# First attention's front rebuilt, its level products made block by block, and the second FFN added straight into the output

## The chip, the cores and the metric

The program runs on one core of a Trainium2 chip. A core has five engines that run side by side and meet only at semaphores: TensorE (PE), VectorE (DVE), ScalarE (ACT), GpSimd (POOL) and SyncE (SP, which only issues transfers here). The metric is the time of one execution in microseconds, smaller being better. The kernel before takes 764.98 us (median of three runs, 763.76 to 766.53).

## The reference

`x` is 2 sequences of 2048 tokens by 128 features, all in float32. Four sublayers follow each other, each added to `x` and each reading the layer-normalised `x`: attention a, an FFN, attention b, the same FFN again.

```python
# attention a (what the change is about)
V = complex(mat_v_real, mat_v_imag)           # 64 x 64
Vinv = inv(V)
a2 = (xf @ w_a.T).reshape(b, l, 64, 2)        # complex pair
a  = a2 as complex * rsqrt(mag2) * sigmoid(log(mag2))
xc = (xf @ w_x.T) as complex * sqrt(mag2)
u  = einsum('mn,bln->blm', Vinv, x_roll)      # x_roll: h0, then xc shifted by one
s  = associative_scan of (a, a * u) along l   # s_t = a_t * (s_{t-1} + u_t)
h  = einsum('mn,bln->blm', V, s) + xc
y  = h.real @ w_out.T
# FFN: each of 16 experts takes its 256 best tokens (top_k over tokens)
xe = xn[idx];  h = gelu(xe @ fc1.T + b1);  y = h @ fc2.T + b2
output = zeros.at[flat_idx].add(y * gates);   output / gate_sums
```

## The kernel before, in words

Everything is written by hand: each engine has its own instruction list and semaphores are counted, so the order on an engine is the order of the code.

**Front of attention a.** The tokens are worked in four blocks `k` of 512 tokens of both sequences. SP loads the four 64x64 parts of `V` and its transpose (eight loads), then the eight groups of `x`, then the weights. DVE makes the statistics of all tokens, ACT one square root (`root(0)`, L470), and then, block by block: DVE normalises into `stage` (L969; two groups, reused, so block k+1 waits for the transposes of block k), PE transposes into PSUM, ACT copies to `xT` (L474, `keep_xT`), PE projects with `waT` into four PSUM banks (L689), ACT squares the four banks (L501), copies them to `av` and `XC` (L507, L508) and takes the square root of the magnitudes (L513). DVE's `coefficients(k)` adds the squares (L1009, `mag`), takes `1/(1+mag)` (L1011, L1012) and scales `XC` and `av` (three products, by the helper at L934).

**The inverse.** `inv(V)` comes from a Newton iteration on the real 128x128 form of `V`, with 24 steps of two links: link one is PE L662 and L664 and ACT L484 (`Zm`), link two PE L668 and L669 and ACT L488 (both copies of `XX`). `inverse(n)` emits links up to number n; calls of it are woven into the blocks on PE and ACT (eight links a block), and the rest follow the last block. DVE then builds `BD` from the result (L1034 to L1039) and prepares bit masks for later (`bits`, ten tiny steps by L934 and L938).

**The scan.** PE makes `u` in five chunks (L709 to L712), DVE folds each chunk with `av` (`U_CHUNKS`), and then goes up and down the ten levels of a tree. The products of coefficients of each level, `lev`, are made by POOL (L385 to L388, four instructions a level) once all of `av` is there (`proj_used` at `NK`); DVE waits for them by `lev_ready`. PE multiplies the result by the output weights (L720), DVE adds it to `x`.

**The FFN** (`feed(f)`, run twice). After the choice of tokens, POOL issues indirect transfers: gathers of an expert's 256 rows from `tab` into the ring `XE` of eight places (L415, two a gather), and scatters of `y` that add into DRAM (L431, two an expert). Seven experts are gathered ahead. Even experts add into `acc[f][0]`, which holds a copy of `x`, odd ones into `acc[f][1]`, which SP has zeroed (L291). A scatter waits for the one two experts before it. DVE makes `y` (L1234, L1237) and waits ahead of it (L1232) for the same scatter. At the end SP reads both arrays back (L314, L318), DVE and POOL add them (L438) and in the second FFN SP stores the sum to `out` (L329).

Of the kernel before, what the change touches and what calls it, by code (L numbers as in the profile page):

```python
# [14 lines left out]
P = 128  # L15
# [22 lines left out]
def build(nc, x, wa, wx, wo, vr, vi, vrT, viT, h0r, h0i, wqkvT, woutT, nw, rwT, rb, f1T, f1b, f2T, f2b, out):  # L38
# [26 lines left out]
    acc = [[nc.dram_tensor(f"acc{f}{i}", [NTOK, D], F32).ap() for i in range(2)] for f in range(2)]  # L65
    cntd = [nc.dram_tensor(f"cntd{f}", [P, GW], F32).ap() for f in range(2)]

    with ExitStack() as ctx:
# [25 lines left out]
        aI = sb("aI", [P, 2, P])  # L94
# [10 lines left out]
        SS = carve(2 * LT).rearrange("p (c t) -> p c t", c=2)  # L105
        XC = carve(2 * (LT + 1)).rearrange("p (c t) -> p c t", c=2)
# [52 lines left out]
        RX = 8  # L159
        XE = carve(RX * 2 * TW).rearrange("p (r h w) -> p r h w", r=RX, h=2)  # L160
# [46 lines left out]
        scattered = [sem(f"scattered{i}") for i in range(2)]  # L207
        acc_in = [sem(f"acc_in{g}") for g in range(NG)]
# [18 lines left out]
        stored = sem("stored")  # L227
# [5 lines left out]
        nw_start, nw_sq, nw_norm, nw_Y, nw_Z, nw_X, nw_new, nw_newT = (sem(s) for s in ("nw_start", "nw_sq", "nw_norm", "nw_Y", "nw_Z", "nw_X", "nw_new", "nw_newT"))  # L233
# [6 lines left out]
        N_WIDE, N_LAST = 18, 6  # L240
        HALVES = 2 * (N_WIDE + N_LAST)
# [4 lines left out]
        WA, WB = 3.5, 3.5 * 3.5 / 4  # L246

# [8 lines left out]

        @block.sync
        def _(sp):
            for t, src in ((RT[0:64, 0:64], vrT), (RT[64:128, 64:128], vrT), (RT[0:64, 64:128], viT), (RT[64:128, 0:64], viT),
                           (Rm[0:64, 0:64], vr), (Rm[64:128, 64:128], vr), (Rm[0:64, 64:128], vi), (Rm[64:128, 0:64], vi)):  # L260
                sp.dma_start(t, src).then_inc(inv_in, 16)
            for g in [b * NK + k for k in range(NK) for b in range(NB)]:
                b, k = divmod(g, NK)
                sp.dma_start(xs[:, g * TPG:(g + 1) * TPG, :],
                             x[b, k * GW:(k + 1) * GW, :].rearrange("(t p) d -> p t d", p=P)).then_inc(x_in[g], 16)
# [23 lines left out]
            for f in range(2):  # L289
                for g in range(NG):  # L290
                    sp.dma_start(acc[f][1][g * GW:(g + 1) * GW, :].rearrange("(p r) w -> p (r w)", r=TPG), zero  # L291
                                 ).then_inc(zeroed, 16)

            def feed(f):
# [4 lines left out]
                for g in range(NG):  # L299
                    sp.dma_start(acc[f][0][g * GW:(g + 1) * GW, :].rearrange("(t p) w -> p t w", p=P),  # L300
                                 xs[:, g * TPG:(g + 1) * TPG, :]).then_inc(base_in, 16)
# [10 lines left out]
                sp.wait_ge(scattered[0], 32 * NE // 2 * (f + 1))  # L312
                for g in range(NG):
                    sp.dma_start(xs[:, g * TPG:(g + 1) * TPG, :], acc[f][0][g * GW:(g + 1) * GW, :].rearrange("(t p) w -> p t w", p=P)  # L314
                                 ).then_inc(acc_in[g], 16)
                sp.wait_ge(scattered[1], 32 * NE // 2 * (f + 1))
                for g in range(NG):
                    sp.dma_start(acc1[:, g * TPG:(g + 1) * TPG, :], acc[f][1][g * GW:(g + 1) * GW, :].rearrange("(t p) w -> p t w", p=P)  # L318
                                 ).then_inc(acc_in[g], 16)
# [3 lines left out]
            for g in range(NG):  # L323
                b, k = divmod(g, NK)
                if g % 2:
                    sp.wait_ge(x_ready_pool, HALF_NG + g // 2 + 1)
                else:
                    sp.wait_ge(x_ready, HALF_NG + g // 2 + 1)
                sp.dma_start(out[b, k * GW:(k + 1) * GW, :].rearrange("(t p) d -> p t d", p=P),  # L329
                             xs[:, g * TPG:(g + 1) * TPG, :]).then_inc(stored, 16)  # L330
            sp.wait_ge(stored, 16 * NG)

        @block.gpsimd
        def _(pool):
# [39 lines left out]
            pool.wait_ge(proj_used, NK)  # L374
            pool.wait_ge(projected, NK)
            lo = 0
            A = av
            for lv in range(1, LEVELS):
                n = LT >> lv
                B = lev[:, :, lo:lo + n]  # L380
                lo += n
                t1 = xT[:, 0:2 * n].rearrange("p (c t) -> p c t", c=2)
                t2 = xT[:, 2 * n:4 * n].rearrange("p (c t) -> p c t", c=2)
# [3 lines left out]
                pool.tensor_tensor(B[:, 0, :], t1[:, 0, :], t2[:, 1, :], ALU.subtract).then_inc(lev_ready, 1)  # L387
                pool.tensor_tensor(B[:, 1, :], t1[:, 1, :], t2[:, 0, :], ALU.add).then_inc(lev_ready, 1)  # L388
                pool.wait_ge(lev_ready, 2 * lv)
                A = B  # L390

            def feed(f):

                pool.wait_ge(zeroed, 16 * NG * 2)
# [13 lines left out]
                def gather(e):  # L408
                    if e == 0:
                        pool.wait_ge(idx_ready, f + 1)  # L410
                    if e >= RX:
                        pool.wait_ge(y_ready, f * NE + e - RX + 1)
                    for h in range(2):
                        i = h * NE + e
                        pool.indirect_dma_start(out=XE[:, e % RX, h, :], out_offset=None, in_=tab[f],  # L415
                                                in_offset=bass.IndirectOffsetOnAxis(ap=idx[:, i:i + 1], axis=0)
                                                ).then_inc(xe_in[e % RX], 16)

                for e in range(RX - 1):
                    gather(e)  # L420
                pool.wait_ge(base_in, 16 * NG * (f + 1))
                for e in range(NE):
                    if e + RX - 1 < NE:
                        gather(e + RX - 1)
                    pool.wait_ge(y_ready, f * NE + e + 1)
                    if f * NE + e >= 2:

                        pool.wait_ge(scattered[e % 2], 32 * ((f * NE + e) // 2))
                    for h in range(2):
                        i = h * NE + e  # L430
                        pool.indirect_dma_start(out=acc[f][e % 2], out_offset=bass.IndirectOffsetOnAxis(ap=idx[:, i:i + 1], axis=0),  # L431
                                                in_=yv[:, e % 2, h, :], in_offset=None, compute_op=ALU.add
                                                ).then_inc(scattered[e % 2], 16)

                for g in range(1, NG, 2):
                    t = slice(g * TPG, (g + 1) * TPG)
                    pool.wait_ge(acc_in[g], 32 * (f + 1))
# [25 lines left out]
        def _(act):  # L463

# [7 lines left out]
            def keep_xT(run, n, g):  # L472
                act.wait_ge(transposed, run * NG + n + 1)
                nc.scalar.activation(xT[:, g * GW:(g + 1) * GW], ps[:, 6 + n % 2, :], ACT.Copy).then_inc(xT_ready, 1)  # L474
# [3 lines left out]
            def inverse(upto):  # L478

                while done[0] < min(upto, HALVES):  # L480
                    i, half = divmod(done[0], 2)
                    if half == 0:
                        act.wait_ge(nw_Y, i + 1)
                        nc.scalar.activation(Zm[:, :], ps[:, 5, 0:P], ACT.Copy).then_inc(nw_Z, 1)  # L484
                    else:
                        act.wait_ge(nw_X, i + 1)
                        for a, ready in enumerate((nw_new, nw_newT)):
# [7 lines left out]
            def squares(k, at):  # L495
                inverse(at + 5)
                act.wait_ge(projected, k + 1)
                if k >= 1:
                    act.wait_ge(mag_ready, k)
# [878 lines left out]
```

## Time and profile before

| quantity | value |
|---|---|
| median of 3 runs | 764.98 us |
| the profiled execution | 773.48 us, its span 771.7 us |
| DVE busy | 471.5 us, 61% of the span |
| PE busy | 434.5 us, 56% |
| POOL busy | 347.9 us, 45% |
| ACT busy | 208.8 us, 27% |
| first attention | 0 to about 192 us |
| second FFN's gathers, experts and end | about 644 us to the end |

No engine is busy all the time: the stages have different limits, and each is read by itself. In the timeline a row gives the start in us, the length in us, the engine, the line of the program, what is written and read, and in brackets how long the engine had been idle and what ended that. In the chain of waits a row is a piece of the one path that ended last. In windows of time an engine's number is its busy time in us, and PEclk is the granted share of TensorE's clock. "Landing" is the time from the issue of a transfer to its completion.

### The profile page before, as it was taken

The page shows a single profiled execution, that of the slowest core. Times are in us where ns is not written, and L with a number is a line of the kernel's source. Part 1 is how long each engine was busy: PE and PEld are TensorE (multiplying, and loading weights), DVE is VectorE, ACT ScalarE, POOL GpSimd, SP SyncE. Part 2 cuts the span into 40 slices and gives each one's busy share as a digit, 9 for nine tenths or more (in the row PEclk, how much of TensorE's full clock was granted, in tenths as well). Part 3 has the DMA queues.
Part 4 walks back from the last instruction along what each step waited for, and adds up shares of the span by engine and source line. Part 5 has one row for each costly group of instructions (what it writes and reads, how often), then busy time and mean ns, then how long its engine had stood idle before and what let it go on. Part 6 is the DMA issues. An engine that isn't in the chain of part 4 may idle for free.

```text
span 771.7 us, 7616 instructions
## 1 busy us (share of the span) xinstructions
PE 434.5 (56%) x2146; PEld 289.0 (37%) x2146; DVE 471.5 (61%) x1205; ACT 208.8 (27%) x511; POOL 347.9 (45%) x330
## 2 busy tenths in 40 slices
PE   4787476008432157778007889888753313887730
PEld 3544344007211056667003334334331102776630
DVE  5475699999777712222066898999967883221211
ACT  2547100000443013223026333323143401232210
POOL 5000790000100066888425877787810004688872
PEclk9999568658855578999558888998976555889975
DMA  4790000000500522333730000000050014233359
GB/s 128 265 400 8 0 0 1 0 0 7 157 0 0 148 52 37 45 45 37 159 79 0 0 1 1 0 1 0 1 163 2 0 47 133 44 45 44 36 84 277
DMA packets 63684, 47.30 MB, mean 61 GB/s; under 512 B 9184, under 2 KB 58976, under 8 KB 62368
## 3 DMA queue, kind: packets, MB, share of 16 engines
q1 hardware_dynamic: 52256, 37.81, 16.1%
q0 software_dynamic: 11392, 9.05, 8.8%
q8 instruction: 17, 0.28, 0.1%
q14 instruction: 19, 0.16, 0.1%
HBM read 26.92 MB, written 19.92 MB: 61 GB/s over the span
## 4 chain that ended last, share of the span: by engine, by line
DVE 24%; POOL 24%; issue 18%; PE 13%; DMA 9%; ACT 5%; SPq 3%; another core or an unknown queue 1%; DVEq 1%; POOLq 0%
POOL acc L431 9%; DVE arena L934 8%; POOL tb L459 8%; DMA acc<-arena,idx 5%; POOL arena L415 4%; DVE tk L939 2%; PE ps L720 2%; DVE arena L939 2%; PE ps L689 2%; DVE tb L969 2%; DMA tab<-tb 2%; PE ps L768 1%; DMA arena<-acc 1%; POOL arena L455 1%
## 5 line engine op out<-in xcount | busy, mean ns | idle before, releaser
L431 POOL DMA_INDIRECT acc<-arena,idx x64 | 101.2, 1581 | 27.6 <-issue 16.2
L934 DVE TENSOR_TENSOR arena<-ps,arena 128x256 f32<-128x256 f32 (+1 forms) x36 | 16.3, 453 | 138.0 <-DMA acc<-arena,idx 115.4
L549 ACT ACTIVATE arena<-ps,b 128x256 f32<-128x256 f32 x128 | 50.1, 474 | 148.1 <-PE ps L820 115.8
L820 PE MATMUL ps<-arena,f1w 128*128 128x256 f32 x256 | 74.5, 442 | 27.7 <-DVE arena L938 23.1
L459 POOL TENSOR_TENSOR tb<-arena 128x512 f32<-128x512 f32 x64 | 80.5, 1271 | 17.0 <-DVE arena L1296 17.0
L867 PE MATMUL ps<-xT,arena 128*128 128x512 f32 x128 | 72.3, 660 | 20.3 <-DVE arena L1296 20.2
L415 POOL DMA_INDIRECT arena<-tab,idx x64 | 62.4, 975 | 41.8 <-DMA tab<-tb 22.9
L830 PE MATMUL ps<-f2w,arena 128*128 128x128 f32 x512 | 68.5, 287 | 7.1 <-issue 7.0
L830 PEld LDWEIGHTS ps<-f2w,arena 128*128 128x128 f32 x512 | 67.4, 203 | 10.7 <-issue 8.1
L820 PEld LDWEIGHTS ps<-arena,f1w 128*128 128x128 f32 x256 | 54.1, 222 | 39.9 <-DVE arena L938 26.9
L934 DVE TENSOR_TENSOR arena<-arena 128x256 f32<-128x256 f32 (+26 forms) x127 | 56.4, 479 | 2.6
L254 POOL DMA_DIRECT2D arena<-cntd x4 | 2.7, 687 | 117.0 <-DMA cntd<-arena 117.0
L720 PE MATMUL ps<-tb,arena 128*128 128x256 f32 x96 | 25.2, 430 | 43.8 <-DVE arena L934 37.8
L385 POOL TENSOR_TENSOR xT<-arena 128x2048 f32<-128x2048 f32 (+9 forms) x10 | 10.7, 1075 | 69.1 <-DVE arena L934 68.4
L396 POOL CAST arena<-ident 128x128 f16<-128x128 f32 x2 | 0.6, 290 | 89.6 <-DVE tb L969 89.6
L939 DVE TENSOR_SCALAR_CACHE_REDUCE arena<-arena,tk 128x320 f16<-128x320 f32 (+1 forms) x66 | 37.1, 564 | 4.7 <-DVE tk L939 2.1
L867 PEld LDWEIGHTS ps<-xT,arena 128*128 128x128 f32 x128 | 22.6, 207 | 44.6 <-DVE arena L1296 36.5
L720 PEld LDWEIGHTS ps<-tb,arena 128*128 128x128 f32 x96 | 20.9, 220 | 48.6 <-DVE arena L934 38.2
L470 ACT ACTIVATE sd<-sd 128x32 f32<-128x32 f32 x4 | 0.9, 229 | 140.6 <-DVE sd L957 140.6
L538 ACT ACTIVATE arena<-arena,tk 128x192 f16<-128x192 f32 x60 | 27.3, 455 | 41.8 <-DVE tk L939 39.6
L1296 DVE TENSOR_TENSOR_SCAN arena<-ones,arena,ps 128x512 f32<-128x512 f32 x30 | 37.3, 1260 | 0.0
L455 POOL TENSOR_TENSOR arena<-arena 128x512 f32<-128x512 f32 x24 | 30.5, 1272 | 8.7 <-ACT arena L608 8.6
(220 smaller groups left out, 948.1 us busy)
## 6 DMA issues: line engine op xcount, KB each, us to landing
tab<-tb SPq DMA_DIRECT2D x8, 576.0 KB, 5.7
f1w<-in_f1T SPq DMA_DIRECT2D x4, 1024.0 KB, 11.0
f2w<-in_f2T SPq DMA_DIRECT2D x4, 1024.0 KB, 13.0
acc<-tb SPq DMA_DIRECT2D x16, 256.0 KB, 12.1
acc<-xs SPq DMA_DIRECT2D x16, 256.0 KB, 6.3
xs<-acc SPq DMA_DIRECT2D x16, 256.0 KB, 5.5
arena<-acc SPq DMA_DIRECT2D x16, 256.0 KB, 5.4
xs<-in_x SPq DMA_DIRECT2D x8, 256.0 KB, 4.9
```

What stands on the lines that cost most here:

```text
L415: pool.indirect_dma_start(out=XE[:, e % RX, h, :], out_offset=None, in_=tab[f], in_offset=bass.IndirectOffsetOnAxis(ap=idx[:, i:i + 1], ax ...
L431: pool.indirect_dma_start(out=acc[f][e % 2], out_offset=bass.IndirectOffsetOnAxis(ap=idx[:, i:i + 1], axis=0), in_=yv[:, e % 2, h, :], in_ ...
L455: pool.tensor_tensor(KV[:, j % 2, :], KV[:, j % 2, :], kn[:, r, :], ALU.mult).then_inc(kv_ready, 1)
L459: pool.tensor_tensor(QS[:, i, :], ST[:, r, i, :], qn[:, r, :], ALU.mult).then_inc(qs_ready, 1)
L549: last = nc.scalar.activation(hT[:, e % 2, t, :], ps[:, 2 * (e % 2) + t // 2, (t % 2) * CAP:(t % 2 + 1) * CAP], ACT.Gelu, bias=b1[:, e, t: ...
L720: return nc.tensor.matmul(ps[:, n, t * 2 * D:(t + 1) * 2 * D], lhs, MB[:, i, :, :].rearrange("p b d -> p (b d)"), start=(i == 2 and t == 0 ...
L820: last = nc.tensor.matmul(ps[:, 2 * (e % 2) + t // 2, (t % 2) * CAP:(t % 2 + 1) * CAP], f1w[:, e, t * P:(t + 1) * P], xeT[:, e % 2, :], st ...
L830: last = nc.tensor.matmul(ps[:, 6 + m % 2, h * P:(h + 1) * P], hT[:, m % 2, t, h * P:(h + 1) * P], f2w[:, m, t, :], start=(t == 0), stop=( ...
L867: nc.tensor.matmul(ps[:, u % V_BANKS, :], WV[:, i, :, :].rearrange("p h a -> p (h a)"), xT[:, n * GW:(n + 1) * GW], start=True, stop=True) ...
L934: return nc.vector.tensor_tensor(o, a, b, op)
L939: return nc.vector.tensor_scalar(o, a, s1, s2, op0, op1, **kw)
L1296: nc.vector.tensor_tensor_scan(ST[:, r, i, :], ones_in.to_broadcast([P, GW]), kv, ST[:, 1 - r, i, GW - 1:GW] if n % NK else 0.0, ALU.mult, ...
```

## The change

- **x on two queues.** ACT issues four of the loads of `V` and the four `x` groups of the first sequence; SP keeps the others. A square root right at the start draws ACT's table load forward. DVE makes the statistics of the first `x` group ahead of the start of the inverse.
- **The front in one go.** All 32 tiles are normalised at once into `XN`, which lies in parts of the arena that are still free, so no block waits for `stage`. The transposes of block k+1 and the squares of block k stand between the projections, the raw copy is made ahead of the squares (which now read SBUF), and all front transposes use bank 7.
- **The inverse in other steps.** Ten pairs of three links (`form`, `square`, `apply`) and two last steps of two links: 34 links, six a block, where there were 48 and eight. The copies into `BD` and `MB` go from DVE to ACT.
- **Level products per block.** POOL makes the first two levels' products of each block when its coefficients are there, the others as before; it waits for `mag_ready` of the next block first.
- **Second FFN into `out`.** `x` is copied to `out`, and all experts of the second FFN add there; each scatter waits for the one just before it. Six experts are gathered ahead instead of seven, and each further gather stands behind a scatter. The reading back, the addition and the store at the end are gone, and so is half of the zeroing.

```diff
-        AT_FIRST, AT_STEP = 7, 8
+        PAIRS = (3.9,) * 8 + (3.4, 2.2)
...
+        AT_ROOT, AT_FIRST, AT_STEP = 8, 12, 6
+
+        BY_BLOCK = 2
...
@@ SP, end of feed(f)
+                if f:
+                    sp.wait_ge(base_in, 16 * NG * 2)
+                    sp.wait_ge(out_scattered, 32 * NE)
+                    return
...
@@ POOL, levels
-            pool.wait_ge(proj_used, NK)
...
+            for k in range(NK):
+
+                pool.wait_ge(proj_used, k + 1)
+                if k + 1 < NK:
+                    pool.wait_ge(mag_ready, k + 2)
+                pool.wait_ge(transposed, min(2 * (k + 2), NG))
+                A = av[:, :, k * GW:(k + 1) * GW]
+                for i in range(BY_BLOCK):
+                    n = GW >> (i + 1)
...
+                    level(A, B, n)
...
@@ POOL, feed(f)
+                def scatter(e):
+                    pool.wait_ge(y_ready, f * NE + e + 1)
+                    if f:
+                        if e:
+                            pool.wait_ge(out_scattered, 32 * e)
...
+                        scatter(e)
+                        for s in range(got, min(got + 2, 2 * NE)):
+                            gather(s)
...
@@ PE, blocks
+                for i in range(2):
...
+                    last.then_inc(projected, 1)
+                    inverse(at + 2 * i + 1)
+                    if k + 1 < NK:
+                        transposes(0, 2 * (k + 1) + i, lambda t: XN[i][k + 1][:, t, :])
+                    inverse(at + 2 * i + 2)
+                inverse(at + 6)
...
@@ DVE
-            norm_a(0)
             for k in range(NK):
-                if k + 1 < NK:
-                    norm_a(k + 1)
+                norm_a(k)
+            for k in range(NK):
                 coefficients(k)
...
-            V.did(nc.vector.tensor_copy(BD[lo_, 0, lo_], XX[lo_, 1, lo_]))
...
```

Three places in the engines' lists. First ACT between the projections of one block and the next (`Zm`, `XX`: the inverse; `arena<-ps 128x2x512`: a raw copy; `tb<-tb`: the square root; `arena<-ps 128x256`: the copy in a pair's middle), before:

```order
L501 ACTIVATE arena<-ps 128x512 x2
L484 ACTIVATE Zm<-ps 128x128
L501 ACTIVATE arena<-ps 128x512 x2
L488 ACTIVATE XX<-ps 128x128 x2
L507 ACTIVATE arena<-ps 128x2x512
L508 ACTIVATE arena<-ps 128x2x512
L484 ACTIVATE Zm<-ps 128x128
L513 ACTIVATE tb<-tb 128x1024
L474 ACTIVATE xT<-ps 128x512
L488 ACTIVATE XX<-ps 128x128 x2
L474 ACTIVATE xT<-ps 128x512
```

The same engine there after the change:

```order
L562 ACTIVATE arena<-ps 128x2x512
L531 ACTIVATE Zm<-ps 128x128
L521 ACTIVATE xT<-ps 128x512
L553 ACTIVATE tb<-tb 128x1024
L569 ACTIVATE arena<-arena 128x1024
L535 ACTIVATE arena<-ps 128x256
L562 ACTIVATE arena<-ps 128x2x512
L539 ACTIVATE XX<-ps 128x128
L541 ACTIVATE XX<-ps 128x128
L521 ACTIVATE xT<-ps 128x512
L569 ACTIVATE arena<-arena 128x1024
```

A raw copy now frees its banks first, and the next block's `xT` stands between the halves of this one. The second place is POOL's first two levels, before:

```order
L385 TENSOR_TENSOR xT<-arena 128x2048 [waits projected,proj_used]
L386 TENSOR_TENSOR xT<-arena 128x2048
L387 TENSOR_TENSOR arena<-xT 128x1024 [waits gstep]
L388 TENSOR_TENSOR arena<-xT 128x1024
L385 TENSOR_TENSOR xT<-arena 128x1024 [waits lev_ready]
L386 TENSOR_TENSOR xT<-arena 128x1024
```

The same work for one of the four blocks after the change:

```order
L395 TENSOR_TENSOR stage<-arena 128x512 [waits mag_ready,proj_used,transposed,lev_ready,gstep]
L396 TENSOR_TENSOR stage<-arena 128x512
L397 TENSOR_TENSOR arena<-stage 128x256 [waits gstep]
L398 TENSOR_TENSOR arena<-stage 128x256
L395 TENSOR_TENSOR stage<-arena 128x256 [waits lev_ready,gstep]
L396 TENSOR_TENSOR stage<-arena 128x256
```

Each block's share is a quarter in size and starts with the block. The third place is POOL's transfers in the second FFN at the first experts, before (`arena<-tab,idx`: half a gather, `acc<-arena,idx`: half a scatter):

```order
L415 DMA arena<-tab,idx 128x144 [waits base_in]
L415 DMA arena<-tab,idx 128x144
L431 DMA acc<-arena,idx 4096x128 [waits scattered0,y_ready]
L431 DMA acc<-arena,idx 4096x128
L415 DMA arena<-tab,idx 128x144 [waits y_ready]
L415 DMA arena<-tab,idx 128x144
L431 DMA acc<-arena,idx 4096x128 [waits scattered1,y_ready]
L431 DMA acc<-arena,idx 4096x128
```

After the change:

```order
L442 DMA arena<-tab,idx 128x144 [waits idx_ready,tab_stored]
L442 DMA arena<-tab,idx 128x144 x11
L455 DMA out<-arena,idx 4096x128 [waits y_ready,base_in]
L455 DMA out<-arena,idx 4096x128
L442 DMA arena<-tab,idx 128x144 x2
L455 DMA out<-arena,idx 4096x128 [waits out_scattered,y_ready]
L455 DMA out<-arena,idx 4096x128
```

Twelve half gathers stand ahead of the first scatter where there were sixteen, and a scatter's wait is now on the one directly before it.

## Rows read from the trace of the kernel before

**Rows 1.** Chain of waits over the span: start us, length us, what.
```profile
25.89 1.87 PE ps L689 x8
...
65.78 1.87 PE ps L689 x8
...
88.53 2.62 DVE BD L1034
...
98.43 2.29 DVE bits L934
```
**Rows 2.** Timeline of the start of the front.
```profile
12.98 0.79 PE L664 MATMUL ps<-XX,RT 128*128 128x128 f32 x2
...
14.14 0.79 PE L668 MATMUL ps<-Zm,XX 128*128 128x128 f32 x2 [0.37 <-ACT Zm L484]
...
15.72 0.79 PE L664 MATMUL ps<-XX,RT 128*128 128x128 f32 x2
...
16.85 1.28 ACT L470 ACT_TABLE_LOAD   x1
...
18.14 0.23 ACT L470 ACTIVATE sd<-sd 128x32 f32<-128x32 f32 x1
```
**Rows 3.** Windows: PE, PEld, DVE, ACT, POOL busy, PEclk, DMA share, GB/s.
```profile
39.00:52.00 13.00, 9.87 (x56) 5.67 (x55) 9.85 (x14) 8.20 (x21) 0.00 (x0) 1.00 1.01 395
...
76.00:88.00 12.00, 10.33 (x36) 7.95 (x36) 6.85 (x8) 3.96 (x14) 5.89 (x2) 0.53 0.00 0
```
**Rows 4.** DVE from 76 to 106 us by shape: busy us, mean ns, idle.
```profile
L1012 DVE RECIPROCAL tb<-tb 128x512 f32<-128x512 f32 x1 | 3.4, 3352 | 0.0
L1034 DVE COPY BD<-XX 64x64 f32<-64x64 f32 x1 | 2.6, 2619 | 5.6 <-ACT XX L488 5.6
L934 DVE TENSOR_TENSOR arena<-arena,tb 128x1024 f32<-128x1024 f32 x2 | 2.5, 1225 | 0.1
...
L1035 DVE COPY BD<-XX 64x64 f32<-64x64 f32 x1 | 0.2, 192 | 0.0
```
**Rows 5.** POOL from 76 to 120 us by shape.
```profile
L385 POOL TENSOR_TENSOR xT<-arena 128x512 f32<-128x512 f32 x1 | 1.3, 1266 | 0.1
...
L387 POOL TENSOR_TENSOR arena<-xT 128x256 f32<-128x256 f32 x1 | 0.7, 727 | 0.1
```
**Rows 6.** Timeline of DVE: the first chunk's fold, and the levels' start.
```profile
105.87 0.75 DVE L934 TENSOR_TENSOR arena<-arena,ps 128x256 f32<-128x256 f32 x2
...
129.04 47.75 DVE L934 TENSOR_TENSOR arena<-arena 128x256 f32<-128x256 f32 x104
```
**Rows 7.** Timeline: last gather ahead and first `y`, in both FFNs.
```profile
290.60 0.94 POOL L415 DMA_INDIRECT arena<-tab,idx  x1 [0.30 <-issue]
...
294.25 0.42 DVE L934 TENSOR_TENSOR arena<-ps,arena 128x256 f32<-128x256 f32 x1 [11.54 <-remote]
...
663.36 0.95 POOL L415 DMA_INDIRECT arena<-tab,idx  x1 [0.30 <-issue]
...
667.03 0.42 DVE L934 TENSOR_TENSOR arena<-ps,arena 128x256 f32<-128x256 f32 x1 [10.98 <-remote]
```
**Rows 8.** Timeline of POOL: first half scatters of two experts, and the last half scatter.
```profile
668.26 1.65 POOL L431 DMA_INDIRECT acc<-arena,idx  x1 [3.95 <-DVE arena L938]
...
674.71 1.63 POOL L431 DMA_INDIRECT acc<-arena,idx  x1 [0.30 <-issue]
...
747.66 1.55 POOL L431 DMA_INDIRECT acc<-arena,idx  x1 [0.30 <-issue]
```
**Rows 9.** Chain of waits from 655 us: from a scatter's issue to its landing.
```profile
689.49 3.30 DMA acc<-arena,idx
...
736.53 4.17 DMA acc<-arena,idx
...
747.66 6.30 DMA acc<-arena,idx
```
**Rows 10.** Timeline of SP: the stores of the result.
```profile
760.49 6.92 SPq L329 DMA_DIRECT2D out<-xs  x8
```

More of the change, by code:

```diff
@@ L64, in build @@
     tab = [nc.dram_tensor(f"tab{f}", [NTOK, TW], F32).ap() for f in range(2)]
-    acc = [[nc.dram_tensor(f"acc{f}{i}", [NTOK, D], F32).ap() for i in range(2)] for f in range(2)]
+    acc = [nc.dram_tensor(f"acc{i}", [NTOK, D], F32).ap() for i in range(2)]
+    outf = out.rearrange("b t d -> (b t) d")
     cntd = [nc.dram_tensor(f"cntd{f}", [P, GW], F32).ap() for f in range(2)]
@@ L322, in _ @@
             feed(1)
[L323 to L331, printed above, removed]
         @block.gpsimd
@@ L419, in feed @@
-                for e in range(RX - 1):
-                    gather(e)
+                        pool.indirect_dma_start(out=outf if f else acc[e % 2],
+                                                out_offset=bass.IndirectOffsetOnAxis(ap=idx[:, i:i + 1], axis=0),
+                                                in_=yv[:, e % 2, h, :], in_offset=None, compute_op=ALU.add
+                                                ).then_inc(out_scattered if f else scattered[e % 2], 16)
+                got = 2 * AHEAD[f]
@@ L421, in feed @@
+                for s in range(got):
+                    gather(s)
                 pool.wait_ge(base_in, 16 * NG * (f + 1))
                 for e in range(NE):
[L423 to L433, printed above, removed]
+                    if f == 0:
+                        for s in range(got, min(got + 2, 2 * NE)):
+                            gather(s)
+                            got += 1
+                        scatter(e)
+                    else:
+                        scatter(e)
+                        for s in range(got, min(got + 2, 2 * NE)):
+                            gather(s)
+                            got += 1
@@ L670, in inverse @@
                     done[0] += 1
+            for b in range(NB):
+                inverse(AT_FIRST - 1 + b)
+                transposes(0, b, lambda t: XN[b][0][:, t, :])
+            pe.wait_ge(wab_in, 32)
             for k in range(NK):
                 at = AT_FIRST + AT_STEP * k
-                for b in range(NB):
-                    inverse(at + b)
-                    if k == 0 and b == 0:
-                        pe.wait_ge(wab_in, 32)
-                    transposes(0, 2 * k + b, lambda t: stage[:, b * TPG + t, :])
```

314 lines of the change are left out of this document (180 added, 134 removed).

## The prediction, made before the changed kernel ran

> **What bounds the kernel now.** I read the chain of waits first, for the places where the end is decided, then the timeline of those two places, then windows and groups by shape for durations. In the front the chain stands on the projections [rows 1]: from 25.89 to 65.78 are three blocks, 13.3 us each. It does not go from there to the scan: it goes over the inverse, whose links run on alone after the last block, to DVE's copies into BD at 88.53, to the bit masks at 98.43, and only at 105.87 does DVE fold the first chunk [rows 6]. From there to about 174 us DVE works without a gap worth naming, so what is won ahead of 105.87 is won for the whole program, since nothing behind it reads a clock. In the second FFN POOL's own issuing is the pace: an expert starts each 6.45 us [rows 8], and POOL's idle time before a scatter is its own 0.30. Then come the landing, the reading back, the sum and the store.
>
> **The front's start: 1.6 us lost.** A Newton step's first link took 1.16 us (12.98 to 14.14) and its second 1.58 (14.14 to 15.72) [rows 2]. A pair of the new kind has a form at 1.16, a square of four products with one wider copy at about 1.65, and an apply at 1.16, since its first product alone releases the next link: 3.97 us. The two queues bring V's parts about 1.8 us sooner, but DVE now makes one group's statistics first and waits for its x, so I let the first link start at 10.4 instead of 9.8. The root stands behind eight links: 10.4 + 2 x 3.97 + 1.16 + 1.65 = 21.15, ending at 21.4, against 18.37 before, although the table load of 1.28 us there is gone [rows 2]. From the root to the first projection it was 7.5 us; with fewer links between, and no wait for stage, I take 6.0: the first projection starts at 27.4 against 25.8.
>
> **The blocks: 6 us won by the last projection.** Per block ACT was busy 8.20 us [rows 3]. Four steps of three copies become two pairs of four, one of them wider: twelve copies of about 0.24 (8.20 us over 21 instructions, the other nine being much longer) against eight of 0.3, so 7.7. The new order makes ACT's list one string: it waits for PE's first projection of the block (1.87, with the wake 2.0) and, at the end, PE waits for the last square and apply (about 1.0). 7.7 + 2.0 + 1.0 = 10.7. Last projection: 27.4 + 3 x 10.7 = 59.5, against 65.8. DVE's part of a block is two products of 1.23, one of 0.68, the sum of 1.23, 0.43 and the reciprocal of 3.35 [rows 4]: 8.2, below 10.7.
>
> **What POOL's blocks cost DVE.** BD's copies of 64x64 took 2.62 us beside a POOL product and 0.19 in a gap between two [rows 4], so DVE stands until POOL's instruction ends. A block's eight POOL instructions are two of 1.27, four of 0.73 and two of about 0.4: 6.2 us; the largest two and the 0.7 are [rows 5], the smallest are an estimate by size. The wait for the next mag keeps the sum of squares free of them and the reciprocal (3.35) covers about half, so the loss a block lies between 0 and 6.2; I take 1.0 to 1.5, most of which the slack of 10.7 - 8.2 swallows in blocks 1 and 2. Only the last block's 0.9 shows. The Trainium skill ("SBUF — State Buffer", on GpSimd and VectorE contention) calls the shared ports an exclusive lock held for the whole instruction, which also binds a product with both inputs in SBUF; the copies agree. By that page every one of the five such instructions of a block could meet a POOL instruction, and the sum would be the third rival's.
>
> **The way to the first chunk.** The last mag comes 8.1 us after the last projection, at 67.6, and av is complete at 67.6 + 8.2 + 0.9 = 76.7 (82.0 before). All 34 links are spent with block 3, so BD is built by ACT near 71, and PE has the first two chunks ready. The whole piece from 82.0 to 98.4, waiting for the inverse and copying BD in POOL's gaps, falls away. What is late next is DVE's own bit masks, 98.43 to 105.87, 7.4 us, mostly waits for POOL: they stay, because POOL starts block 3's products at the same moment. First chunk: 76.7 + 7.4 = 84.1 instead of 105.87, 21.8 us earlier. The folds of the five chunks took 23.2 us (105.87 to 129.04) [rows 6] while POOL finished small levels; now it has larger ones beside them, for which I charge 1.4 (bounds 0 and 4). **Front: 20.4 us won.** Level products are not a wait: from 83 POOL needs some 15 us more, and DVE takes up the levels at 108.6.
>
> **The second FFN, its start.** DVE stood 10.98 us until the first y at 667.03, and the profile names no engine for it ("remote"); in the first FFN it was 11.54 us at the same place [rows 7]. In both FFNs the first y comes 3.65 and 3.67 us after the last gather ahead was issued [rows 7]; though the idle times differ by over 0.5. I read that something these engines need stands behind the gathers. Twelve half gathers instead of sixteen, at 1.25 us each, end the stall 5.0 us earlier, and the first scatter starts at 663.3 instead of 668.3. Bounds: 0 and 5, since no more than the four gathers can be taken out.
>
> **Its pace.** Ten experts still have a gather behind their scatter: 6.43 us. The second half scatter is issued 1.93 us after the first and lands 3.3 to 4.2 us later [rows 9]; 1.93 + 3.4 + 0.3 = 5.65 is hidden under 6.43. For the last six experts it is not hidden: 5.65 instead of 3.7 each (two half scatters at 1.55 + 0.30 [rows 8]). First scatter at s, last one's start at s + 10 x 6.43 + 5 x 5.65 = s + 92.6, its landing at + 1.93 + 3.4 = s + 97.9, that is 761.2 for s = 663.3. The end was 771.7: a last landing of 6.30 us, the reads, the sum and the stores (760.49 + 6.92 and their landing) [rows 9, 10] are gone. **10.3 us won**; serialising alone costs about 10, the end gives back 18.
>
> **Small edits at nothing.** Half the zeroing (under the blocks), x copied to out instead of acc (lands while the choice runs), MB's copies on ACT (after BD, needed by chunk 1 only). If the cover of MB were gone: 1 us.
>
> **Sum.** 20.4 + 10.3 = 30.7. Against the profiled execution's span, 771.7 - 30.7 = 741.0. The profiled execution is 8.5 us above the median of the runs; I take the same difference off the median: 764.98 - 30.7 = 734.3, told as 734.
>
> **Rivals.**
> 1. *The stall is not tied to the gathers* (a fixed wait that begins with the first experts). The first scatter stays at 668.3, the FFN gives 5.3: 739. For it: the gathers start at the same point too, so two equal cases can't part the two. 24%.
> 2. *PE's clock stays at the lower level in the blocks.* In the blocks before, the granted clock was 1.00, and it fell to 0.53 (1.2 GHz of 2.4) when only links ran [rows 3]; the new blocks hold the same products in less time, which speaks against it. With all products at the lengths of 13 us (0.79 where a fast one is about 0.49 by the ratio of the levels), a block's two projections cost 2 x 1.16 more and the links and transposes in its string about 1.1: 4 x 3.4 = 13.6 us: 748. 4%.
> 3. *DVE becomes the bound of the blocks.* All of POOL's 6.2 us fall on it: 14.4 a block instead of 10.7, 3 x 3.7 = 11 us: 745. Against: the reciprocal covers half. 12%.
> 4. *The front starts at full speed.* Denser links bring the quick level before the first transposes: 3.7 us less, 730 or 731. 7%.
> 5. *Slower: every scatter into one array lands as late as the last one.* That one took 6.30 us [rows 9]. Each expert then costs 1.93 + 6.3 + 0.3 = 8.53; 663.3 + 15 x 8.53 + 8.2 = 799.5, 27.8 later than 771.7; with the front's 20.4 that is 772. It decides from a landing of 5.9 us on. Against: nearly all scatters landed in 3.3 to 4.3, and the late one ran beside eight reads of acc. 3%.
>
> My own case has 50%, and its range is 731 to 738. **Range 726 to 747**: down past the fourth rival with both bounds at their good end, up to the third. Within 0.3% (2.3 us) a measurement of this kernel can't tell a change. Faster by more: all but the fifth rival and a remnant, 0.95; within it 0.02; slower 0.03.
>
> **What the profile after would show.** Right: three distances of about 10.7 between first projections; BD written by ACT near 71, before the last coefficients; DVE's first chunk at 84; POOL products of 512 beside each block; the first y of the second FFN at 3.7 us after its twelfth half gather; scatters at 6.4 and then 5.7 us. Wrong: distances above 12 (rivals 2 and 3, told apart by PEclk and by the length of DVE's products of 1.23); a first y that comes 22.5 us after the first gather again (rival 1); waits before scatters while gathers are still left (rival 5).

## The result, and the profile after

The changed kernel takes 736.9 us (median of 4 runs, 735.7 to 738.6) beside 765.8 us of the kernel before in the same session (763.8 to 768.5): a ratio of 0.9623, 95% interval 0.9597 to 0.9649, or 28.8 us less. I had predicted 734 and a gain of 30.7 us, 20.4 in the front and 10.3 in the second FFN. The profiled execution after took 735.7 us, its span is 733.9.

The chain of waits in the front (start, length, what), which answers to [rows 1]:
```profile
24.41 1.94 PE ps L770 x8
...
35.16 1.87 PE ps L770 x8
...
45.85 1.87 PE ps L770 x8
...
56.54 1.89 PE ps L770 x8
...
64.50 1.39 DVE tb L1098
66.37 3.36 DVE tb L1101
69.76 1.49 DVE arena L1021
71.25 1.14 DVE tb L1021
72.42 1.63 DVE arena L1021
75.01 1.18 DVE bits L1021
```
The first projections are 10.7 us apart (13.3 before). The copies into BD have left the chain; only DVE's bit masks stand between the last product of av and the first fold. The links at the start, PE's timeline, against [rows 2]:
```profile
9.52 0.80 PE L731 MATMUL ps<-arena,ident 128*128 128x128 f32 x2 [1.08 <-DVE nrm L1080]
...
12.92 0.80 PE L753 MATMUL ps<-arena 128*128 128x128 f32 x2 [0.47 <-ACT arena L535]
13.51 0.45 PE L754 MATMUL ps<-arena 128*128 128x128 f32 x2
...
14.08 0.49 PE L733 MATMUL ps<-XX,RT 128*128 128x128 f32 x2
...
16.98 0.49 PE L733 MATMUL ps<-XX,RT 128*128 128x128 f32 x2
```
From 13.5 us the same products take 0.39 to 0.49 us instead of 0.63 to 0.80, and a pair of links takes 2.90 us (14.08 to 16.98). The first pair, nearly all of it at the long lengths, took 3.97 (10.11 to 14.08), which is the length I had taken for all of them. DVE's bit masks and folds, and its take-up of the levels, against [rows 6]:
```profile
73.97 0.43 DVE L1021 TENSOR_TENSOR bits<-ione,ish 128x32 uint32<-128x32 uint32 x1
...
74.82 0.15 DVE L1025 TENSOR_SCALAR bits<-bits 128x1 uint32<-128x1 uint32 x1
75.01 1.17 DVE L1021 TENSOR_TENSOR bits<-bits 128x1 uint32<-128x1 uint32 x1
...
78.92 0.75 DVE L1021 TENSOR_TENSOR arena<-arena,ps 128x256 f32<-128x256 f32 x2
...
103.37 2.81 DVE L1021 TENSOR_TENSOR arena<-arena 128x256 f32<-128x256 f32 x3
```
The levels start 25.7 us earlier than in [rows 6]. A mask operation over one element a partition takes 1.17 us and ends with POOL's product of 512 (74.91 to 76.17), where the one before it, with a single input, takes 0.15: most of the 1.17 is a wait. In the second FFN, the first y on DVE and then POOL's last gather ahead, first scatter and last two half scatters ([rows 7, 8]):
```profile
627.83 0.42 DVE L1021 TENSOR_TENSOR arena<-ps,arena 128x256 f32<-128x256 f32 x1 [3.48 <-PE ps L917]
```
```profile
626.68 0.94 POOL L442 DMA_INDIRECT arena<-tab,idx  x1 [0.30 <-issue]
630.21 1.66 POOL L455 DMA_INDIRECT out<-arena,idx  x1 [2.59 <-issue]
...
724.67 1.55 POOL L455 DMA_INDIRECT out<-arena,idx  x1 [2.44 <-DMA out<-arena,idx]
726.53 1.55 POOL L455 DMA_INDIRECT out<-arena,idx  x1 [0.31 <-issue]
```
The first y is worked 1.15 us after the last gather ahead was issued, not 3.65, and DVE waits for PE, no longer for something "remote". The chain at the end shows the serial steps of the last experts, and what follows the last issue:
```profile
714.73 3.34 DMA out<-arena,idx
718.11 0.71 issue
718.83 1.55 POOL out L455
720.37 0.30 issue
720.68 3.24 DMA out<-arena,idx
...
724.67 1.55 POOL out L455
```

### The profile page after: what moved, and what is told of

Read it like the earlier page. It is cut to its first block, busy times and chain, and to the rows that moved or that the text cites. A ratio compares the mean times of both kernels' runs of the same rounds, so it can differ in the third digit from the quotient of the medians.

```text
span 733.9 us, 7537 instructions
## 1 busy us (share of the span) xinstructions
PE 410.8 (56%) x2130; PEld 273.7 (37%) x2130; DVE 461.8 (63%) x1199; ACT 205.2 (28%) x487; POOL 355.6 (48%) x350
## 4 chain that ended last, share of the span: by engine, by line
DVE 27%; POOL 22%; issue 17%; DMA 15%; PE 13%; ACT 4%; SPq 1%; DVEq 1%; ACTq 0%; POOLq 0%
DVE arena L1021 10%; POOL tb L501 8%; DMA out<-arena,idx 5%; DMA acc<-arena,idx 5%; POOL acc L455 4%; POOL out L455 4%; POOL arena L442 3%; DVE tk L1026 2%; PE ps L807 2%; DVE arena L1026 2%; PE ps L770 2%; DVE tb L1056 2%; DMA tab<-tb 2%; PE ps L855 2%; POOL arena L497 1%
## 5 line engine op out<-in xcount | busy, mean ns | idle before, releaser
L501 POOL TENSOR_TENSOR tb<-arena 128x512 f32<-128x512 f32 x64 | 80.4, 1270 | 17.2 <-DVE arena L1369 17.2
L442 POOL DMA_INDIRECT arena<-tab,idx x64 | 62.6, 978 | 41.5 <-DMA tab<-tb 22.6
L917 PEld LDWEIGHTS ps<-f2w,arena 128*128 128x128 f32 x512 | 64.2, 197 | 4.4 <-issue 2.2
L917 PE MATMUL ps<-f2w,arena 128*128 128x128 f32 x512 | 63.9, 279 | 2.0 <-DVE arena L1025 2.0
L907 PEld LDWEIGHTS ps<-arena,f1w 128*128 128x128 f32 x256 | 53.8, 221 | 27.4 <-DVE arena L1025 14.4
L455 POOL DMA_INDIRECT out<-arena,idx x32 | 50.9, 1590 | 23.5 <-issue 10.5
L455 POOL DMA_INDIRECT acc<-arena,idx x32 | 50.6, 1580 | 9.7 <-issue 7.0
L891 PE MATMUL ps<-ident,arena 128*128 128x128 f32 x64 | 14.4, 311 | 37.8 <-DMA arena<-tab,idx 29.9
```

The lines of the kernel that those rows point to most:

```text
L455: pool.indirect_dma_start(out=outf if f else acc[e % 2], out_offset=bass.IndirectOffsetOnAxis(ap=idx[:, i:i + 1], axis=0), in_=yv[:, e % 2 ...
L501: pool.tensor_tensor(QS[:, i, :], ST[:, r, i, :], qn[:, r, :], ALU.mult).then_inc(qs_ready, 1)
L907: last = nc.tensor.matmul(ps[:, 2 * (e % 2) + t // 2, (t % 2) * CAP:(t % 2 + 1) * CAP], f1w[:, e, t * P:(t + 1) * P], xeT[:, e % 2, :], st ...
L917: last = nc.tensor.matmul(ps[:, 6 + m % 2, h * P:(h + 1) * P], hT[:, m % 2, t, h * P:(h + 1) * P], f2w[:, m, t, :], start=(t == 0), stop=( ...
```

## The experiments

Three sessions, each on another chip and each with its own runs of the kernel before: 772.3 us in the first, 764.8 in the second, 765.1 in the third. Ratios are always to the runs of the same session. That the kernel before is 7 us slower in the first turned out to be the key to one of the questions.

The theories after the result: the front gained more than predicted, the second FFN less, and the stall at the first y was tied to something other than the gathers, or was not there at all.

**First session.** `before_again`, the kernel before unchanged:

> The kernel before, profiled once more. Theory A (the 11 us in which VectorE stood for the first y of each FFN belonged to that one profiled execution, not to the kernel): the first y comes 14 to 16 us after the first gather with no long idle time before it, the first scatter right behind the 16th half gather (20.1 us after the first), and the span is 771.7 - 7.3 = 764 us. Theory B (the stall belongs to the kernel, as the prediction had it): first y again 22.5 us after the first gather in both FFNs, span near 771 us.

It took 2149 us in its one run (PE busy 91% of the span, a product of 128x512 3.0 us in the mean instead of 0.66), a disturbed execution that tells nothing here.

`front_only`, the changed front with the second FFN of before; the main part kept from before, in words (the zeroing, the reading back, the sum and the store are as before too):
```
-                    if f:  scatter(e) into outf, wait out_scattered; AHEAD 6
+                    gather(e + RX - 1); scatter(e) into acc[f][e % 2]; AHEAD 7
```


> The changed front (x on two queues, blocks, inverse, levels per block) with the second FFN of the kernel before. The prediction's sum gives 20.4 us for it (744.6 us). The trace after, where DVE starts the levels at 103.37 instead of 129.04, gives 25.5 us (739.5 us). If the two parts of the change lean on each other, neither holds and the two single gains don't add up to 28.8 us.

Measured: 749.2 us, ratio 0.9688 (0.9663 to 0.9713), 23.1 us won. The interval is 22.2 to 26.0 us: it holds the 25.5 of the trace and not the 20.4 of the prediction.

`ffn_only`, the kernel before with the new second FFN alone; the edit is the one above turned round:

> The kernel before with the second FFN's part alone (experts added into out, each scatter behind the one before it, six experts gathered ahead, no reading back). The prediction: 10.3 us (754.7 us), 5.0 of them from a stall that ends earlier. Theory A (no such stall in timed executions): the first scatter comes only 2.7 us earlier, the serial scatters cost 10 and the end gives back, so 2 to 4 us in all (761 to 763 us).

Measured: 767.9 us, ratio 0.9944 (0.9925 to 0.9964): 4.4 us won, where I had put 10.3. From the first gather of the second FFN to the end of the span it took 122.8 us against 127.2 in the kernel before.

`levels_after`, the changed kernel with all of POOL's levels after the last block:
```
                 A = av[:, :, k * GW:(k + 1) * GW]
-                for i in range(BY_BLOCK):
-                    n = GW >> (i + 1)
...
-                    level(A, B, n)
...
-            for lv in range(BY_BLOCK + 1, LEVELS):
+            scratch = xT[:, :]
+            for lv in range(1, LEVELS):
```


> The changed kernel, but POOL makes the products of all levels after the last block, as before, in instructions of up to 4.5 us. Theory C (the per-block products matter by what DVE's bit masks and first folds wait for at the shared port): the masks take 10 to 16 us instead of 4.9, the last coefficients get 1 us shorter, DVE starts the levels 7 to 12 us later: 744 to 749 us. Theory D (they only bring POOL's work forward, DVE never waited for levels): no difference from the changed kernel, 737 us, or up to 3 us less since the blocks are free of POOL.

Measured: 756.9 us, ratio 0.9798 (0.9776 to 0.982). The first gather of the first FFN came at 259.28 us against 246.23 in the changed kernel: 13 us, so the levels made beside the blocks are half of what the front won. POOL's products are now up to 4.5 us long, and DVE's timeline shows where the time goes:
```profile
72.82 0.15 DVE L1020 TENSOR_SCALAR bits<-bits 128x1 uint32<-128x1 uint32 x1
73.01 4.25 DVE L1016 TENSOR_TENSOR bits<-bits 128x1 uint32<-128x1 uint32 x1
...
86.47 0.76 DVE L1016 TENSOR_TENSOR arena<-arena,ps 128x256 f32<-128x256 f32 x2
87.26 4.14 DVE L1016 TENSOR_TENSOR arena<-arena 128x128 f32<-128x128 f32 x2
...
115.61 10.26 DVE L1016 TENSOR_TENSOR arena<-arena 128x256 f32<-128x256 f32 x9
```
The ten mask operations last 14.1 us (72.41 to 86.47) instead of 4.9, as theory C had it, and the folds 29.1 instead of 24.5; the last coefficients are ready 1.6 us earlier. So DVE takes up the levels 12.2 us later. Among masks and folds only the operations with two inputs in SBUF wait: those with a single input take 0.15 us, and those that read one input from PSUM (`arena<-arena,ps`) 0.76, as in the changed kernel. (BD's copies, with one input, did wait [rows 4].)

All three had the stall at the first y: 11.5, 11.3 and 11.5 us in the first FFN. In the second, `front_only` (seven experts ahead) had 11.0, the two with six ahead 5.3. DVE in `ffn_only`, with POOL's last gather ahead and first scatter:
```profile
658.80 0.42 DVE L946 TENSOR_TENSOR arena<-ps,arena 128x256 f32<-128x256 f32 x1 [5.33 <-remote]
```
```profile
655.77 0.95 POOL L412 DMA_INDIRECT arena<-tab,idx  x1 [0.31 <-issue]
661.19 1.66 POOL L425 DMA_INDIRECT out<-arena,idx  x1 [4.47 <-issue]
```
DVE starts on the first y 3.03 us after the last gather ahead was issued (3.67 with sixteen half gathers) and 16.9 us after the first gather (22.6 with sixteen). But the scatter then waits 1.45 us after y is done (659.74) where it waited 0.29 before, for nothing that the profile names; so it comes 19.33 us after the first gather instead of 23.78: 4.4 us, where the prediction has 5.0 for the same edit. With the stall present, it does end with the gathers.

**Second session.** `after_again`, the changed kernel unchanged:

> The changed kernel itself, unchanged. In its profiled execution the first y of neither FFN had waited: DVE's idle time there was 3.0 and 3.5 us, put down to PE, where the kernel before and three kernels with parts of the change showed 11.3 to 11.5 us (FFN 1), 11.0 us (FFN 2, seven experts ahead) and 5.3 us (FFN 2, six ahead), put down to no engine. Theory S (the stall is a matter of the execution or the chip, not of this kernel's code): it comes back here, about 11.4 us in FFN 1 and 5.3 us in FFN 2, from first gather to first scatter 23.7 and 19.3 us. Theory K (the changed kernel as a whole has no stall, since something in its front and its second FFN together takes it away): 20.1 and 17.4 us again. Ratio 0.962 by the earlier comparison.

Measured: 738.3 us, ratio 0.9645 (0.9619 to 0.9672). No stall: from first gather to first scatter 20.12 and 17.59 us. That speaks for theory K, or for a chip on which nothing has the stall; the two are told apart in the third session.

`bits_early`, the bit masks moved:
```
             for k in range(NK):
                 norm_a(k)
+            dve.wait_ge(consts, 3)
+            V.step(tt(bits[:, 0:32], ione[:, :], ish[:, :], ALU.logical_shift_left))
...
             for k in range(NK):
                 coefficients(k)
```


> The changed kernel with DVE's ten small bit-mask instructions ahead of the first block's coefficients, where DVE waits for the first squares, instead of between the last product of av and the first fold (73.97 to 78.89 us in the trace of the changed kernel, 4.9 us). If the folds wait for nothing else, the first starts at 74.0 and the whole program is 4.5 to 5 us shorter than the changed kernel (ratio to the kernel before 0.956). Rival: PE's first chunk product is not ready at 74, since BD was copied by 68.4 and PE has MT and the chunk's products after it; then 1 to 3 us. Slower is not expected: the ten small instructions take 1 to 2 us in DVE's wait ahead of the blocks.

Measured: 734.8 us, ratio 0.9599 (0.9571 to 0.9626), 3.5 us below `after_again`; the intervals overlap, the traces agree in sign. DVE's timeline, with a mask, the last product of av, the first folds and the start of the levels:
```profile
28.91 0.16 DVE L1021 TENSOR_TENSOR bits<-bits 128x1 uint32<-128x1 uint32 x1
...
72.12 1.63 DVE L1021 TENSOR_TENSOR arena<-arena,tb 128x1024 f32<-128x1024 f32 x1
73.68 0.74 DVE L1021 TENSOR_TENSOR arena<-arena,ps 128x256 f32<-128x256 f32 x2
74.45 1.58 DVE L1021 TENSOR_TENSOR arena<-arena 128x128 f32<-128x128 f32 x2
...
100.41 4.71 DVE L1021 TENSOR_TENSOR arena<-arena 128x256 f32<-128x256 f32 x4
```
At 28.3 us POOL is idle, and all ten masks are done in 1.9 us. Counted from the first projection of the last block (56.25 and 56.54), the first fold is 4.95 us earlier, the levels only 2.7 (100.41 and 103.37). The fold follows the last product without a gap, so the masks had covered no wait; but the folds now lie beside POOL's larger products and take 26.7 us instead of 24.5. The 1.58 us above were 1.06.

`ahead7`, seven experts ahead in the second FFN:
```
-        AHEAD = (RX - 1, RX - 2)
+        AHEAD = (RX - 1, RX - 1)
```


> The changed kernel with seven experts' gathers (fourteen half gathers) issued ahead in the second FFN instead of six, still one array. Theory G (the stall is tied to the gathers issued ahead and lasts 3.65 us past the last): the first scatter comes 2 x 1.25 = 2.5 us later, nine experts then have a gather behind their scatter instead of ten, which gives back at most 0.6 us; 1.9 to 2.5 us slower than the changed kernel, if the stall is there. Theory F (the stall is fixed, or absent as in the changed kernel's profiled execution): the first scatter waits for the fourteenth gather or for y, whichever is later, 0 to 0.8 us later than with twelve; within 1 us of the changed kernel.

Measured: 735.6 us, ratio 0.9616 (0.9587 to 0.9644). First gather to first scatter 17.66 us (17.42 and 17.59 with six), first gather to the end of the span 121.3 us (121.1, 121.3): nothing. The fourteenth half gather is issued by 17.35 us after the first, about where the first scatter stands with twelve. The median is 2.8 us below that of `after_again`, which this doesn't explain; see the clock at the end.

`one_queue`, V's parts and x all on SP's queue:
```
+                sp.dma_start(t, src).then_inc(inv_in, 16)
             for k in range(NK):
+                load_x(sp, k)
                 load_x(sp, NK + k)
...
-                act.dma_start(t, src).then_inc(inv_in, 16)
...
-                load_x(act, k)
```


> The changed kernel with all of V's parts and of x on SP's queue instead of on SP's and ACT's. In the profiled execution of the changed kernel the links start at 9.5 us. Eight issues more stand ahead of x on SP (0.6 to 0.8 us each in the kernel before for V's parts), and ACT's own queue is free. Theory: V lands 1.8 us later, as the prediction had it, and the links, which run as one chain to the first projection (24.4 us), move by the same: 1.5 to 2 us slower. Rival: x lands later still (the last group 3 to 5 us), and the statistics of all groups, not the links, set the first projection: 3 to 5 us slower.

Measured: 739.6 us, ratio 0.9659 (0.9634 to 0.9684). The links start at 10.91 us instead of 9.35, the first projection at 25.98 instead of 24.48: 1.5 us, the first theory. The medians differ by 1.3 us, less than either interval can tell; the traces carry it.

**Third session.** `before_traced`, the kernel before unchanged, for its trace:

> The kernel before, unchanged, for its trace. So far its median was 765 us where the changed kernel and three variants of it ran without the stall at the first y, and 772 us where three kernels with parts of the change ran with it; its own profiled execution took 773.5 us and had it. Theory S (the stall is there in some processes or on some chips and absent in others, whatever the kernel): where the median of before is about 765, its trace shows no stall either: first y's idle time about 3 to 4 us in both FFNs, 20.1 us from first gather to first scatter instead of 23.8, and a span near 764. Where the median is about 772, stall of 11 us, span near 771. Theory K (the changed kernel removes it): 23.8 us in both FFNs whatever the median.

Measured: 765.2 us, ratio 1.0 (0.9969 to 1.003). DVE's first two y of the second FFN, then POOL's last gather ahead and first scatter:
```profile
657.84 0.42 DVE L934 TENSOR_TENSOR arena<-ps,arena 128x256 f32<-128x256 f32 x1 [3.67 <-PE ps L830]
661.57 0.42 DVE L934 TENSOR_TENSOR arena<-ps,arena 128x256 f32<-128x256 f32 x1 [2.33 <-PE ps L830]
```
```profile
661.55 0.94 POOL L415 DMA_INDIRECT arena<-tab,idx  x1 [0.30 <-issue]
662.80 1.65 POOL L431 DMA_INDIRECT acc<-arena,idx  x1 [0.30 <-DVE arena L938]
```
y is done before the last gather is issued, and 20.13 us lie between first gather and first scatter, in both FFNs, instead of 23.75 and 23.78. The same kernel, without the stall: theory S. The code doesn't decide on the stall. Whether the chip does or the session is open, since each chip was used in one session only. The trace on which I predicted has it; the runs shown beside it (765.0) have the time of a kernel without it.

`ffn_only_again` and `levels_after_again`, the two kernels of the first session unchanged:

> The kernel before with the second FFN's part alone, again (0.9944 where before took 772 us). Theory S, on a chip without the stall: before loses 3.65 us of wait in each FFN, this kernel 3.65 and 1.9; the part's gain falls from 4.4 us to 2.6 or 2.7 (ratio 0.9965). Theory K: stall as it was, gain 4.4 us, ratio 0.994.

> The changed kernel with all levels made by POOL after the last block, again (0.9798 where before took 772 us). By traces its first gather came at 259.3 us against 246.2 in the changed kernel, 13.1 us later. Beside the changed kernel of this chip state (0.9645 and 0.9623) it should stand at 0.962 to 0.9645 + 13.1 / 765 = 0.979 to 0.982. Theory S: no stall where before takes 765, and first gather to first scatter 20.1 and 17.5 us; theory K with the products per block as the cause: 23.7 and 19.3 us again.

Measured: 760.9 us, ratio 0.9956 (0.9933 to 0.9979), and 750.5 us, ratio 0.9809 (0.9773 to 0.9845). Neither has the stall here (17.27 and 17.76 us from first gather to first scatter of the second FFN), with the code that had it in the first session (19.33 and 19.29). The part's interval holds both 0.9965 and 0.994, so the time alone tells nothing; from first gather to the end of the span it is 121.5 us against 123.4.

`bits_ahead7`, both edits of the second session in one kernel:

> The two variants that were not slower than the changed kernel, together: bit masks early (0.9599) and seven experts ahead in the second FFN (0.9616, against 0.9623 and 0.9645 of the changed kernel). Bit masks: 3.5 to 5 us by trace. Seven ahead: 0 by trace (first y, not POOL, sets the first scatter with twelve half gathers: last gather 626.7, scatter 630.2), and one step of 5.9 for one of 6.4 in exchange: 0 to 0.5 us. Together ratio 0.957 to 0.960, 732 to 734 us beside 765. Where the stall is present, seven ahead costs 2 us and it comes out near 0.960 to 0.962.

Measured: 732.7 us, ratio 0.9578 (0.9549 to 0.9607), the best of all, some 3 to 5 us below the changed kernel (0.9623 and 0.9645). By the trace of `ahead7`, the gain is that of the bit masks. No run parts it from `bits_early` (0.9599): the intervals overlap.

## Why the prediction came out as it did

The time lay in the likeliest case's own range, but that is partly luck: two errors stand in the sum and cancel. The front was priced 5.3 us too low, the second FFN 8.0 us too high.

**The front: 25.7 us by trace, 20.4 predicted.**
- *Start.* It was 3.0 us shorter than predicted (first projection at 24.41, not 27.4). The step that failed is "a pair of the new kind ... 3.97 us" for all links: from the first link to the end of the root it took 9.6 us (9.52 to 19.08) instead of 11.0. A further 0.9 comes from the links' start (9.52 for 10.4) and 0.7 from the way from the root to the projection (5.3 for 6.0). The granted clock reads 1.00 from 9 to 24 us in both traces and doesn't tell the two lengths apart. This is the fourth rival (7%), priced at 3.7 us; the short products are worth between 1.4 and 2.1. What brings them on isn't shown by an experiment, but it goes with the new links: in all nine traces of the new front the links' products have become short by 15.8 us, in the four undisturbed ones of the old front they are still long at 22.4 us.
- *Blocks.* Right: 10.71 us each (24.41 to 56.54 is three), BD built by ACT from 66.87 on (71 predicted). The third rival's clash is there (1.49 and 1.63 us for products of 1.23 [rows 4]), and the slack swallows it as argued; av is complete 17.5 us after the last block's first projection (17.2 predicted).
- *Bit masks.* Step wrong: "they stay", at 7.4 us. They took 4.9. The same ten operations last 1.9 us with POOL idle (`bits_early`), 4.9 in the changed kernel, 6.0 in `before_traced`, 7.4 in the trace that I read, and 14.1 beside POOL's products of 4.5 us (`levels_after`). A wait for another engine's instruction is not a constant that moves along. `bits_early` shows that they need not be on the path at all: I had seen 7.4 us, mostly of waits, and costed an edit that makes them the last thing before the folds, without asking whether they have to stand there.
- *Folds.* Right in size: 24.45 us against 24.6. But they too depend on what POOL does beside them: 22.4 us in `before_traced`, 26.7 in `bits_early`, 29.1 in `levels_after`.

3.0 and 2.5, less 0.3 for av and 0.15 more for the folds, are the 5.3.

**The second FFN: 2.3 us by trace, 10.3 predicted** (first gather to the end of the span: 123.4 in `before_traced`, 121.1 in the changed kernel).
- *The stall, 5.0 us.* The mechanism was right and its presence was not. In the session with the stall the first scatter is 4.4 us earlier; in those without it 2.7 (20.13 to 17.42), since DVE starts on the first y 15.0 us after the first gather, is done with it at 16.0, and the scatter follows 1.4 us later. 2.3 us of the 10.3. The clue stood in the prediction's own sum: the profiled execution was 8.5 us above the median of the runs, and I subtracted that as a constant. Two stalls of 3.65 us are 7.3 of the 8.5.
- *The pace, 5.65 us for the last steps.* They took 6.28, 5.83, 6.27, 5.95 and 5.84, in the mean 6.03: 1.9 us in all. The chain above gives most of it: 1.55 + 0.30 + 3.3 and then 0.71 of issue, for which I had 0.30. The ten steps at 6.43 were right.
- *The end, 5.3 us after the last expert's start.* It took 9.2 (724.67 to 733.9): half scatter, landing, and then 3.9 us more. The prediction puts the end of the program at the last landing. The ends of the two kernels, before and then after (PE, PEld, DVE, ACT, POOL busy, PEclk, DMA share, GB/s):
```profile
768.00:770.00 2.00, 0.00 (x0) 0.00 (x0) 0.00 (x0) 0.00 (x0) 0.00 (x0) 0.50 0.83 248
770.00:772.00 2.00, 0.00 (x0) 0.00 (x0) 0.00 (x0) 0.00 (x0) 0.00 (x0) 0.50 0.02 5
```
```profile
728.00:731.00 3.00, 0.00 (x0) 0.00 (x0) 0.00 (x0) 0.00 (x0) 0.08 (x1) 0.50 0.25 22
731.00:734.00 3.00, 0.00 (x0) 0.00 (x0) 0.00 (x0) 0.00 (x0) 0.00 (x0) 0.50 0.00 0
```
The old end isn't like this: in the three undisturbed traces that end with SP's stores the last traffic is 1.2 to 1.5 us before the end of the span, in all ten that end with scatters 4.2 to 4.8. So most of the 3.9 comes with the new ending. What fills it isn't shown: no engine computes, and SP's last wait (3.8 us, 0.7 before) is put down to PE's queue.

2.3 + 1.9 + 3.9 = 8.1, against 8.0 missing. (The prediction's own terms, 771.7 less 761.2, give 10.5 and not 10.3.)

In the first session the parts alone bring 23.1 and 4.4 us; in the others the whole brings 26.5 to 28.8. The fifth rival is refuted: landings stayed at 3.2 to 3.7 us with one array. The 0.8 us that is left between 28.8 and 25.7 + 2.3 is below what the traces can tell, for the reason given at the end on the clock.

## What to carry to other kernels

Before a trace is used for a sum, compare its own time with the median of the runs. A difference like the 1.1% here can be a wait or a clock that one of them has and the other has not, so find its place before pricing an edit there. A removed tail need not be worth its length: measure both ends at the same kind of event, and don't take the last landing for the end of the program. A wait for a neighbour's long instructions changes its length when moved; where tiny instructions stand in it, put them where the neighbour is idle, and look at what moves into their place.

## What the runs showed of the chip

**A stall that the code doesn't decide.** In the stalled executions the unit that waits is not DVE alone. PE's timeline of the kernel before, as first profiled, with DVE and ACT at its end:
```profile
663.44 0.19 PEld L830 LDWEIGHTS ps<-f2w,arena 128*128 128x128 f32 x1 [0.79 <-issue]
...
665.54 0.19 PEld L830 LDWEIGHTS ps<-f2w,arena 128*128 128x128 f32 x1 [1.20 <-issue]
...
667.03 0.42 DVE L934 TENSOR_TENSOR arena<-ps,arena 128x256 f32<-128x256 f32 x1 [10.98 <-remote]
667.17 1.57 ACT L549 ACTIVATE arena<-ps,b 128x256 f32<-128x256 f32 x4 [7.56 <-remote]
```
PE's products trickle, one in 0.7 us, and DVE and ACT go on together 0.14 us apart, though PE had finished the product for the first y at 659.8. It ends 3.0 to 3.7 us after the last gather ahead in each of the four traces that have it, of four different kernels. What is queued behind the gathers isn't shown by any row, and stays open. The gathers' own data has arrived by 665.5 us, and the one packet of the instruction queue in this stretch comes about 10 us after the first gather in this trace and in `before_traced`, which has no stall.

**TensorE's clock in the first blocks.** In three traces (`before_traced`, `after_again`, `one_queue`) one of the early projections took 3.2 to 3.6 us instead of 1.9. Windows of `after_again` and of the changed kernel (PE, PEld, DVE, ACT, POOL busy, granted clock, DMA share, GB/s):
```profile
33.00:36.00 3.00, 2.19 (x10) 1.53 (x12) 2.79 (x3) 1.22 (x5) 0.00 (x0) 0.80 1.02 431
36.00:42.00 6.00, 6.00 (x30) 2.84 (x28) 2.72 (x2) 3.21 (x5) 0.00 (x0) 0.82 1.00 377
```
```profile
33.00:36.00 3.00, 2.27 (x13) 1.39 (x15) 2.86 (x3) 1.09 (x5) 0.00 (x0) 1.00 1.02 431
36.00:42.00 6.00, 5.93 (x39) 3.55 (x36) 4.34 (x4) 4.90 (x8) 0.00 (x0) 1.00 1.00 379
```
The same code, with a granted clock between the two levels (0.80 and 0.82) in the one and at 2.4 GHz in the other. It costs 1.3 us in that projection and 1.65 from the first block's projections to the last block's. In `before_traced` the row doesn't show it: the granted clock reads 1.00 from 24 to 32 us, and the projection that starts at 26.54 takes 3.61. The start of the front has the same contradiction. A length of a known product says more than the column. From the first gather of the first FFN to that of the second, executions without the stall take 366.2 to 366.6 us or 368.4 to 369.0, whatever the kernel. In the traces of the changed kernel and `after_again` the difference comes up in the second attention, between 125 and 290 us after the first gather; what makes it there isn't shown. The two together fit the 2 to 4 us by which runs of one kernel spread, though only one execution of each was traced, and the 2.8 us between `ahead7` and `after_again`. Edits of 1 us need the trace.
